# State-space stage of a graph network: its turns written out, and the order of work inside a turn changed

## The chip, the cores and the metric

The kernel is one program on one core of a Trainium2 chip. The metric is device time in microseconds (us) from launch to end. The engines are named as in the profile: PE is TensorE (matmuls), PEld its weight loads, DVE is VectorE, ACT is ScalarE, POOL is GpSimd, SP is SyncE, which here issues the DMAs. They run on their own and meet at semaphores.

## The reference, cut to what matters

The whole computes eight layers over 128 graphs of 40 nodes with 128 features. The change touches the second one, `L0_ffn`, alone: nodes are gathered softly into 64 slices, the slices go through a state-space model that runs in both directions, and come back to the nodes.

```python
fx = (x @ W_fx.T + b_fx)                       # per head: 8 heads of 64
xm = (x @ W_x.T + b_x)
sw = softmax((xm @ W_slice.T + b_slice) / temp)    # node -> slice weights ("logits", softmax)
snorm = sw.sum(2)                                  # slice sums
st = einsum('bhnc,bhng->bhgc', fx, sw) / (snorm + 1e-05)[..., None]
# _hydra(st): input projection, convolution, silu, two scans along the 64 slices
#   h = h * dA_t + dBx_t ; y_t = h . C_t           (written as weights W = decays * (B.C) here)
y  = y + x_og * repeat(x_og @ fcD_w.T + Dp, P)
yg = y * silu(z)
yg = yg * rsqrt(mean(square(yg)) + 1e-05) * norm_w # square sums, root, scales
ot = yg @ out_w.T                                  # output projection
out = einsum('bhgc,bhng->bhnc', ot, sw)            # back to the nodes
x = x + out @ out_w.T + out_b                      # to features
```

## The kernel before

`l0_ffn` (L1947) works on 16 chunks (`NCH`) of 8 graphs. In a chunk there are 4 pairs of graphs (`CHP`); a chunk's slices are 512 columns. Three chunks are in work at a time: turn c ends chunk c, takes chunk c+1 through the middle, and begins chunk c+2. Turns run from -2 to 15, so there are 18. `all_turns` (L2153) writes turns -2, -1, 14 and 15 out and has the other fourteen in a hardware loop of seven passes, each with an even and an odd turn in its body; every engine has this loop and a branch at its end (L2156). In the loop, chunk numbers in semaphore waits are register values.

Each engine does the steps of a turn in a fixed order, its list `turn`. TensorE's is:

1. `slices(c+1)`: 128 small matmuls (L2254), 16 transposes of the softmax weights (L2246), which ScalarE copies out (L2401);
2. `input_projection(c+1)`: 10 groups of 4 matmuls (L2280 the first, then L2278); it waits until VectorE has scaled all states (`states`, L2531, semaphore `u_out`) and ScalarE made half of its copies;
3. `mix(c)` (L2320), `steps_down(c+1)` (L2291, L2293), `gains(c+1)` (L2301, L2302; the B-C products), `logits(c+2)` (L2225, L2226);
4. `squares(c)` (L2328), which waits for VectorE's square sums; `output_projection(c)` (L2338), four groups q of 4 matmuls into banks 4 and 5 in turn, of which group 2 waits for ScalarE's copy 0 and group 3 for copy 1 (L2467);
5. `slice_sums(c+2)` (L2239), which waits for the end of the softmax (`smd`); `back_to_nodes(c)` (L2350), `dt_down(c+1)` (L2307), `to_features(c)` (L2358).

VectorE's: `states(c+1)`, the scans (`decayed`, `weights`) of chunk c, `convolve(c+1)`, `gate(c)` (L2591), `square_sums(c)` (L2596, L2598; it waits for ScalarE's squares), `biases(c+2)` (L2498, L2499; each pair waits for its logits), `scales(c)` (L2602; waits for the root), `softmax(c+2)` (maximum L2506, subtraction L2508, then, after ScalarE's exponentials, sum L2510, reciprocal, product L2514), `inverses(c+2)` (L2519, L2521; waits for the slice sums), `nodes(c)`, `out(c)` (L2612; waits for to_features), `columns(c+1)`.

ScalarE's: `slices`, `projected`, `steps_down` of c+1, then `squares(c)` (L2452), `root(c)` (L2456), `out_copy(c, 0)`, `exps(c+2)` (L2392), `out_copy` 1 to 3, `nodes(c)`.

SP's: `load_xn`, `spread_decays(c+1)`, `spread_inverses(c+2)`. The last writes the inverses of the slice sums to memory in 4 DMAs (L2190) and, once these are there, reads them back spread over the partitions in 8 (L2196); `states` of the next turn waits for these pair by pair.

Of the kernel before, what the change touches and what calls it, by code (L numbers as in the profile page):

```python
# [9 lines left out]
ALU = mybir.AluOpType  # L10
# [1936 lines left out]
def l0_ffn(nc, g):  # L1947


    with nc.cleanup_on_exit(), ExitStack() as ctx:  # L1950
# [193 lines left out]
        def there(k):  # L2144

            return not isinstance(k, int) or 0 <= k < NCH
# [4 lines left out]
                eng.wait_ge(sem, value)  # L2151

        def all_turns(eng, turn):  # L2153
            turn(-2, 0)
            turn(-1, 1)
            with eng.Fori(0, (NCH - 2) // 2) as i:  # L2156
                turn(2 * i, 0)
                turn(2 * i + 1, 1)
            turn(NCH - 2, 0)
            turn(NCH - 1, 1)  # L2160

        block = ctx.enter_context(nc.Block())

# [44 lines left out]
        def _(pe):  # L2208
# [19 lines left out]
            def slice_sums(k):  # L2228

                pe.wait_ge(s["smd"], k + 1)  # L2230
                wait(pe, s["xt_out"], 4 * k)
                if there(k - 2):
                    pe.wait_ge(s["ot_out"], 4 * (k - 2) + 3)
                for par in range(2):
                    for f in range(2):
                        o = PS[4][32 * (2 * par + f):32 * (2 * par + f + 1), 0:2 * SG].rearrange("p (k n) -> p k n", k=2)
                        for q in range(CHP):
                            rhs = sw[:, q, :].rearrange("p (f k a n) -> p f a k n", f=2, a=2, n=SG)[:, f, par]
                            mm = pe.matmul(o, selS[:, q, :], rhs, start=(q == 0), stop=(q == CHP - 1))  # L2239
                mm.then_inc(s["sn_ps"], 1)  # L2240
# [87 lines left out]
                    mm = pe.matmul(PS[7][:, 448 + q:449 + q], sq[:, 0, q * 128:(q + 1) * 128], g.mean_w[:, 0:1], start=True, stop=True)  # L2328
                mm.then_inc(s["r_ps"], 1)

            def output_projection(k):
                if there(k + 1):
                    pe.wait_ge(s["xt_out"], 4 * k + 8)
                for q in range(CHP):
                    if q >= 2:
                        pe.wait_ge(s["ot_out"], 4 * k + q - 1)
                    for t in range(KT):
                        mm = pe.matmul(PS[4 + q % 2][:], yg[:, t, q * 128:(q + 1) * 128], wo[:, t, :], start=(t == 0), stop=(t == KT - 1))  # L2338
                    mm.then_inc(s["ot_ps"], 1)
# [12 lines left out]
                    mm.then_inc(s["o_ps"], 1)  # L2352

            def to_features(k):
                pe.wait_ge(s["oT_out"], 2 * k + 2)
                pe.wait_ge(s["oT_act"], 2 * k + 2)
                for t in range(KT):
                    mm = pe.matmul(PS[6][:, 0:CH], wout[:, t, :], oT[:, t].rearrange("p q j n -> p (q j n)"), start=(t == 0), stop=(t == KT - 1))  # L2358
                mm.then_inc(s["f_ps"], 1)

            def turn(c, par):
                if there(c + 1):
                    slices(c + 1)
                    input_projection(c + 1)
                if there(c):
                    mix(c)
                if there(c + 1):
                    steps_down(c + 1)
                if there(c + 1):
                    gains(c + 1)  # L2370
                if there(c + 2):
                    logits(c + 2)
                if there(c):
                    squares(c)
                    output_projection(c)
                if there(c + 2):
                    slice_sums(c + 2)
                if there(c):
                    back_to_nodes(c, par)
                if there(c + 1):  # L2380
                    dt_down(c + 1)
                if there(c):
                    to_features(c)
# [3 lines left out]
        def _(act):  # L2387
# [75 lines left out]
            def out_copy(k, q):  # L2463
                act.wait_ge(s["ot_ps"], 4 * k + q + 1)
                if q == 0:
                    act.wait_ge(s["rms"], k + 1)
                act.activation(ot[:, q, :], PS[4 + q % 2][:], ACT.Copy, scale=rms[:, q:q + 1]).then_inc(s["ot_out"], 1)  # L2467

            def turn(c, par):
                if there(c + 1):  # L2470
                    slices(c + 1, 1 - par)
                    projected(c + 1, 1 - par)
                if there(c + 1):
                    steps_down(c + 1)
                if there(c):
                    squares(c)
                    root(c)
                    out_copy(c, 0)
                if there(c + 2):
                    exps(c + 2)  # L2480
                if there(c):
                    for q in range(1, CHP):
                        out_copy(c, q)
                    nodes(c)
            all_turns(act, turn)
# [2 lines left out]
        def _(dve):  # L2488
# [10 lines left out]
                    dve.tensor_tensor(fx[:, q, :], PS[2 + q % 2][:], bfx[:], ALU.add).then_inc(s["lg_out"], 1)  # L2499
                dve.drain()  # L2500

            def softmax(k):

                sw3 = sw[:].rearrange("p q (h n) -> p (q h) n", n=SG)
                bc = sst[:, :, None].broadcast_to([128, CHP * SH_, SG])
                dve.tensor_reduce(sst[:], sw3, AX.X, ALU.max)  # L2506
                dve.drain()
                dve.tensor_tensor(sw3, sw3, bc, ALU.subtract).then_inc(s["smx"], 1)  # L2508
                dve.wait_ge(s["sme"], k + 1)
                dve.tensor_reduce(sst[:], sw3, AX.X, ALU.add)  # L2510
                dve.drain()
                dve.reciprocal(sst[:], sst[:])
                dve.drain()
                dve.tensor_tensor(sw3, sw3, bc, ALU.mult).then_inc(s["smd"], 1)  # L2514

            def inverses(k):

                dve.wait_ge(s["sn_ps"], k + 1)
                dve.tensor_scalar(rn[:], PS[4][:, 0:2 * SG], 1e-5, None, ALU.add)  # L2519
                dve.drain()  # L2520
                dve.reciprocal(rn[:], rn[:]).then_inc(s["rn"], 1)  # L2521

# [77 lines left out]
            def scales(k):  # L2600
                dve.wait_ge(s["rt"], k + 1)
                dve.reciprocal(rms[:], rms[:]).then_inc(s["rms"], 1)  # L2602
# [25 lines left out]
            def turn(c, par):  # L2628
                if there(c + 1):
                    states(c + 1)  # L2630
                if there(c):
                    decayed(c, 0)
                if there(c + 1):
                    dt_ready(c + 1)
                if there(c):
                    dve.drain()
                    decayed(c, 1)
                    weights(c)
                if there(c + 1):
                    convolve(c + 1)  # L2640
                if there(c):
                    gate(c, par)
                    square_sums(c)
                if there(c + 2):
                    biases(c + 2)
                if there(c):
                    scales(c)
                if there(c + 2):
                    softmax(c + 2)
                if there(c + 2):  # L2650
                    inverses(c + 2)
                if there(c):
                    nodes(c)
                    out(c)
                if there(c + 1):
                    columns(c + 1)
# [98 lines left out]
```

## Time and profile before

| | us |
|---|---|
| three runs | 3872.6, 3874.0, 3877.59 |
| median | 3874.0 |
| the profiled execution | 3859.76 |
| its span, first to last instruction | 3857.9 |
| mean granted TensorE clock | 0.871 |

The page gives, for each engine, its busy time and its share of the span, then the span in 40 slices with a digit for each engine, and the granted clock of TensorE (PEclk, tenths of 2.4 GHz). A slice is 96.4 us; turns 0 to 14 of the state-space stage lie in the fifth to the sixteenth or so. A matmul of 32-bit numbers has two records here, so a row "x8" of 128x512 matmuls is one group of four. In the order of time and in the table of groups, the idle time in square brackets or behind the bar is that just before the instruction, with what ended it; "issue" is time in which the engine waited for nothing that the profile shows.

### The profile page before, as it was taken

To read this page: it belongs to the slowest core of one execution; us is meant where nothing else is said; L and a number is where in the kernel's file an instruction comes from. 1 tells how busy PE (TensorE), PEld (TensorE's weight loads), DVE (VectorE), ACT (ScalarE), POOL (GpSimd) and SP (SyncE) were. 2 spreads that over 40 slices of the span, in tenths; PEclk is the share of its full clock that TensorE was granted. 3 is DMA by queue.
4 is the path that set the end of the run, shared out by engine and by line. 5 is a ranking of instruction groups with operands and counts; after the bars stand their busy time and mean duration, and the time that the engine had idled before them with its cause. 6 is when DMAs were issued, how large, how long until landed. Compare 5 with 4: busy or idle time off the path is not lost. (4 is left out here: it accounts for less than half of the span.)

```text
span 3857.9 us, 56708 instructions
## 1 busy us (share of the span) xinstructions
PE 3137.0 (81%) x21385; PEld 1980.1 (51%) x21385; DVE 2420.5 (63%) x4174; ACT 1336.8 (35%) x2519; POOL 234.5 (6%) x196
## 2 busy tenths in 40 slices
PE   6357999999999999535549995789885988986998
PEld 5224555555555555324426663556552655653665
DVE  6636767777767776399673334488895345773333
ACT  3223434344434344110434443312111444543444
POOL 0000000000000000000000000033221004320000
PEclk7678999999999999755769997699997987897999
DMA  3121121112111112100013321000000212102322
GB/s 38 48 82 37 37 51 37 37 38 59 37 40 48 37 37 51 46 13 1 29 32 78 78 55 15 5 1 0 1 0 26 69 39 51 41 22 58 75 68 68
DMA packets 145000, 152.62 MB, mean 40 GB/s; under 512 B 66628, under 2 KB 124896, under 8 KB 142328
## 3 DMA queue, kind: packets, MB, share of 16 engines
q1 hardware_dynamic: 144800, 149.72, 16.0%
q8 instruction: 154, 2.52, 0.3%
q14 instruction: 46, 0.38, 0.0%
HBM read 141.26 MB, written 8.44 MB: 39 GB/s over the span
## 5 line engine op out<-in xcount | busy, mean ns | idle before, releaser
L812 DVE TENSOR_TENSOR f_hg<-f_hs,f_gb 128x640 f32<-128x640 f32 x320 | 263.7, 825 | 507.6 <-ACT f_hs L794 448.5
L2278 PE MATMUL hy_ps<-hy_uT,hy_win 128*128 128x512 f32 x1152 | 498.7, 594 | 0.0
L794 ACT ACTIVATE f_hs<-f_ph,f_b1t 128x320 f32<-128x320 f32 x640 | 335.1, 527 | 406.2 <-PE f_ph L762 402.2
L762 PE MATMUL f_ph<-XNP,f_w 128*128 (+1 forms) x1280 | 404.8, 440 | 12.9 <-PEq L644 8.6
L777 PE MATMUL f_po<-f_hg,f_w 128*128 128x320 f32 x1280 | 404.9, 439 | 8.9 <-DVE f_hg L812 8.9
L2278 PEld LDWEIGHTS hy_ps<-hy_uT,hy_win 128*128 128x128 f32 x1152 | 217.6, 190 | 281.2 <-issue 281.2
L762 PEld LDWEIGHTS f_ph<-XNP,f_w 128*128 128x128 f32 x1280 | 247.3, 194 | 117.5 <-issue 18.8
L777 PEld LDWEIGHTS f_po<-f_hg,f_w 128*128 128x128 f32 x1280 | 240.4, 191 | 126.4 <-issue 21.3
L2338 PE MATMUL hy_ps<-hy_wo,hy_yg 128*128 128x512 f32 x512 | 227.4, 603 | 0.0
L1803 PE MATMUL er_c<-XNG 128*128 128x400 f32 x544 | 204.6, 516 | 22.4 <-POOL XNG L1734 22.1
L1748 ACT ACTIVATE er_OT<-er_t 128x384 bf16<-128x384 f32 x128 | 61.1, 490 | 309.1 <-PE er_t L1773 309.1
L2338 PEld LDWEIGHTS hy_ps<-hy_wo,hy_yg 128*128 128x128 f32 x512 | 97.7, 193 | 117.0 <-issue 117.0
L2544 DVE TENSOR_TENSOR_SCAN XNG<-XNG,hy_fx 128x2048 f32<-128x2048 f32 x32 | 141.6, 4425 | 2.9 <-issue 1.1
L1783 PE MATMUL er_g<-er_TP,er_OT 128*128 128x320 bf16 x768 | 133.0, 312 | 10.5 <-ACT er_OT L1748 6.1
L1803 PEld LDWEIGHTS er_c<-XNG 128*128 128x128 f32 x544 | 98.7, 194 | 83.0 <-POOL XNG L1734 25.5
L1734 POOL TENSOR_TENSOR XNG<-er_VW,er_MD 128x400 f32<-128x400 f32 x136 | 122.4, 900 | 296.0 <-DVEq L1704 197.2
L2401 ACT ACTIVATE hy_swT<-hy_ps 64x160 f32<-64x160 f32 x256 | 76.4, 299 | 136.8 <-PE hy_ps L2246 133.4
L236 ACT ACTIVATE n_xt<-n_i 128x512 f32<-128x512 f32 x70 | 40.0, 594 | 219.7 <-PE n_i L199 218.7
L207 PE MATMUL n_o<-ident,n_xt 128*128 128x128 f32 x280 | 54.9, 345 | 71.8 <-DVE n_xt L290 71.7
L199 PE MATMUL n_i<-ident,XT 128*128 128x128 f32 x280 | 49.3, 332 | 78.4 <-PEq L2666 28.0
L2418 ACT ACTIVATE hy_xr<-hy_ps 128x512 f32<-128x512 f32 x80 | 47.5, 594 | 177.1 <-PE hy_ps L2278 177.1
L1094 PEld LDWEIGHTS g_ps<-ident,g_P 40*40 40x40 f32 x2048 | 83.2, 128 | 40.6 <-issue 35.7
(520 smaller groups left out, 5506.6 us busy)
## 6 DMA issues: line engine op xcount, KB each, us to landing
f_gb<-gate_rows SPq DMA_DIRECT2D x32, 1280.0 KB, 8.5
XNG<-hy_decays SPq DMA_DIRECT2D x32, 1024.0 KB, 9.5
hy_rb<-hy_inverse SPq DMA_DIRECT2D x128, 128.0 KB, 3.1
f_gb<-gate_rows SPq DMA_DIRECT2D x16, 640.0 KB, 5.1
g_KB<-g_keys SPq DMA_DIRECT2D x32, 320.0 KB, 4.5
hy_xn<-XNP SPq DMA_DIRECT2D x1, 4096.0 KB, 12.5
hy_XC<-hy_xn SPq DMA_DIRECT2D x16, 256.0 KB, 3.4
XNG<-in_L_ffn_edge_index_dram SPq DMA_DIRECT2D x2, 2048.0 KB
```

The source lines that it names most:

```text
L762: pe.matmul(psh[e % 2][k][:], w1[:, e, k * 128:(k + 1) * 128], chunk_view(g, c), start=True, stop=True).then_inc(h_ps, 1)
L777: mm = pe.matmul(pso[par][:], w2[:, e * H2 + k, :], hg[:, e % 2, k, :], start=False, stop=(e == E - 1 and k == H2 - 1))
L794: ins = act.activation(hs[:, e % 2, k, :], psh[e % 2][k][:], ACT.Gelu, bias=b1t[:, e * H2 + k:e * H2 + k + 1])
L812: dve.tensor_tensor(hg[:, e % 2], hs[:, e % 2], gb[:, par, e, None, :].broadcast_to([128, H2, CH]), ALU.mult).then_inc(hg_ready, 1)
L1094: mm = pe.matmul(pst[n % 2][j][rows(j), h, :], P[rows(j), c % 2, h, q, :], g.ident[rows(j), rows(j)], start=True, stop=True)
L1734: pool.tensor_tensor(X[:, u % XBUF], VW[:, 1 - par, u, :, None].broadcast_to([128, V, TJ]), MD[:, 1 - par, u, None, :].broadcast_to([128, ...
L1783: pe.matmul(o[:, 0:NS], OT[:, u % 2, j, :], TP[:, i, j * NS:(j + 1) * NS], start=(i == 0 and j == 0), stop=(i == 2 and j == J - 1))
L1803: mm = pe.matmul(flat(acc[j][:]), OD[:, 1 - par, u, j * 128:(j + 1) * 128], flat(X[:, u % XBUF]), start=False, stop=False, skip_group_chec ...
L2278: mm = pe.matmul(p[:], win[:, t, m * 128:(m + 1) * 128], uT[:, t, :], start=(t == 0), stop=(t == KT - 1))
L2338: mm = pe.matmul(PS[4 + q % 2][:], yg[:, t, q * 128:(q + 1) * 128], wo[:, t, :], start=(t == 0), stop=(t == KT - 1))
L2401: ins = act.activation(o, p[:, :, j, 0:N], ACT.Copy)
L2544: dve.tensor_tensor_scan(L[:, a][:, st], dAb[:, a][:, st], E[:, st], 0.0, ALU.mult, ALU.add)
```

## The change

All turns are written out, and the loop is gone. On TensorE `logits(c+2)` goes ahead of `gains(c+1)`; `output_projection` takes a range of groups, and `slice_sums(c+2)` stands between its third group and its last; the sums go to bank 6 instead of 4, so they no longer wait for the output copies, and `to_features`, which writes bank 6, waits for the inverses (`rn`). On ScalarE the exponentials go ahead of all four output copies. On VectorE `biases(c+2)` goes ahead of `square_sums(c)`, and `scales(c)` stands inside the softmax, after its subtraction. No operation is added or left out.

```diff
         def all_turns(eng, turn):
-            turn(-2, 0)
-            turn(-1, 1)
-            with eng.Fori(0, (NCH - 2) // 2) as i:
-                turn(2 * i, 0)
-                turn(2 * i + 1, 1)
-            turn(NCH - 2, 0)
-            turn(NCH - 1, 1)
+            for c in range(-2, NCH):
+                turn(c, c % 2)
@@ TensorE, slice_sums
                 wait(pe, s["xt_out"], 4 * k)
-                if there(k - 2):
-                    pe.wait_ge(s["ot_out"], 4 * (k - 2) + 3)
-                        o = PS[4][32 * (2 * par + f):32 * (2 * par + f + 1), 0:2 * SG].rearrange("p (k n) -> p k n", k=2)
+                        o = PS[6][32 * (2 * par + f):32 * (2 * par + f + 1), 0:2 * SG].rearrange("p (k n) -> p k n", k=2)
@@ TensorE, output_projection
-            def output_projection(k):
+            def output_projection(k, groups):
-                for q in range(CHP):
+                for q in groups:
@@ TensorE, to_features
+                if there(k + 2):
+                    pe.wait_ge(s["rn"], k + 3)
@@ TensorE, turn
+                if there(c + 2):
+                    logits(c + 2)
                 if there(c + 1):
                     gains(c + 1)
-                if there(c + 2):
-                    logits(c + 2)
                 if there(c):
                     squares(c)
-                    output_projection(c)
+                    output_projection(c, range(CHP - 1))
                 if there(c + 2):
                     slice_sums(c + 2)
                 if there(c):
+                    output_projection(c, range(CHP - 1, CHP))
                     back_to_nodes(c, par)
@@ ScalarE, turn
                     root(c)
-                    out_copy(c, 0)
                 if there(c + 2):
                     exps(c + 2)
                 if there(c):
-                    for q in range(1, CHP):
+                    for q in range(CHP):
@@ VectorE, softmax and inverses
-            def softmax(k):
+            def softmax(k, meanwhile):
                 dve.tensor_tensor(sw3, sw3, bc, ALU.subtract).then_inc(s["smx"], 1)
+                meanwhile()
                 dve.wait_ge(s["sme"], k + 1)
-                dve.tensor_scalar(rn[:], PS[4][:, 0:2 * SG], 1e-5, None, ALU.add)
+                dve.tensor_scalar(rn[:], PS[6][:, 0:2 * SG], 1e-5, None, ALU.add)
@@ VectorE, turn
                     gate(c, par)
-                    square_sums(c)
                 if there(c + 2):
                     biases(c + 2)
                 if there(c):
+                    square_sums(c)
+                if there(c + 2):
+                    softmax(c + 2, lambda: scales(c) if there(c) else None)
+                    inverses(c + 2)
+                else:
                     scales(c)
-                if there(c + 2):
-                    softmax(c + 2)
-                if there(c + 2):
-                    inverses(c + 2)
```

## Rows read from the trace of the kernel before

**Rows 1.** The page: busy time, share of the span, instructions.
```profile
PE 3137.0 (81%) x21385; PEld 1980.1 (51%) x21385; DVE 2420.5 (63%) x4174; ACT 1336.8 (35%) x2519; POOL 234.5 (6%) x196
```

**Rows 2.** Windows, output projection to output projection: busy per engine, clock, DMA.
```profile
383.00:1465.40 1082.40, 1037.28 (x8219) 573.60 (x8218) 792.97 (x899) 432.79 (x767) 0.00 (x0) 0.97 0.17 43
...
883.20:964.20 81.00, 77.58 (x634) 42.77 (x634) 60.87 (x70) 33.30 (x59) 0.00 (x0) 1.00 0.17 44
1048.90:1131.00 82.10, 78.85 (x633) 42.98 (x634) 60.98 (x70) 33.29 (x59) 0.00 (x0) 0.98 0.17 43
```

**Rows 3.** Waits of TensorE, 400 to 1500 us: total, times, longest.
```profile
PE hy_ps L2254 <- issue: 17.6, 12, 1.8
PE hy_ps L2280 <- DVE hy_uT L2531: 14.8, 8, 2.9
PE hy_ps L2246 <- ACT hy_swT L2401: 4.3, 8, 0.5
PE hy_ps L2280 <- ACT hy_swT L2401: 4.2, 5, 1.8
```

**Rows 4.** TensorE in time, boundary after turn 5 (branch): start, duration.
```profile
822.98 1.97 PE L2254 MATMUL hy_ps<-hy_sw,hy_fx 40*64 40x64 f32 x89 [1.25 <-issue]
826.51 1.64 PE L2254 MATMUL hy_ps<-hy_sw,hy_fx 40*64 40x64 f32 x39 [1.56 <-issue]
```

**Rows 5.** TensorE in time, boundary after turn 6 (no branch).
```profile
909.76 0.63 PE L2246 MATMUL hy_ps<-ident,hy_sw 128*128 128x128 f32 x4 [0.54 <-ACT hy_swT L2401]
912.13 3.63 PE L2280 MATMUL hy_ps<-hy_uT,hy_wdt 128*40 128x512 f32 x8 [1.75 <-ACT hy_swT L2401]
```

**Rows 6.** VectorE in time, turn 6 and the states after it.
```profile
875.65 1.23 DVE L2596 TENSOR_TENSOR hy_uT<-hy_uT 128x1024 f32<-128x1024 f32 x1 [4.86 <-ACT hy_uT L2452]
...
883.24 0.68 DVE L2499 TENSOR_TENSOR hy_fx<-hy_ps,hy_bfx 128x512 f32<-128x512 f32 x1
...
890.90 2.29 DVE L2510 TENSOR_REDUCE hy_sst<-hy_sw 128x32 f32<-128x2048 f32 x1 [2.17 <-ACT hy_sw L2392]
...
893.69 2.29 DVE L2514 TENSOR_TENSOR hy_sw<-hy_sw,hy_sst 128x2048 f32<-128x2048 f32 x1
899.65 0.29 DVE L2519 TENSOR_SCALAR hy_rn<-hy_ps 128x128 f32<-128x128 f32 x1 [3.67 <-PE hy_ps L2239]
...
911.33 0.76 DVE L2531 TENSOR_TENSOR hy_uT<-hy_ps,hy_rb 128x256 f32<-128x256 f32 x2 [0.54 <-DMA hy_rb<-hy_inverse]
```

**Rows 7.** TensorE in time, gains to output projection of turn 6.
```profile
872.65 0.33 PE L2301 MATMUL hy_ps<-hy_Cs,hy_xs 64*64 64x64 f32 x4
...
874.90 1.10 PE L2225 MATMUL hy_ps<-hy_wlg,hy_XC 128*128 128x512 f32 x2
...
878.89 1.12 PE L2225 MATMUL hy_ps<-hy_wlg,hy_XC 128*128 128x512 f32 x2 [0.32 <-DVE hy_fx L2499]
...
881.57 1.02 PE L2226 MATMUL hy_ps<-hy_wfx,hy_XC 128*128 128x512 f32 x2
882.43 0.95 PE L2328 MATMUL hy_ps<-mean_w,hy_uT 128*128 128x1 f32 x8
883.24 13.98 PE L2338 MATMUL hy_ps<-hy_wo,hy_yg 128*128 128x512 f32 x32
```

**Rows 8.** ScalarE in time, copies of the transposes after turn 6.
```profile
908.39 4.99 ACT L2401 ACTIVATE hy_swT<-hy_ps 64x160 f32<-64x160 f32 x16 [5.83 <-PE hy_ps L2246]
```

**Rows 9.** Windows (columns as rows 2) where the clock was low.
```profile
825.00:831.80 6.80, 5.28 (x56) 4.68 (x55) 3.85 (x9) 2.45 (x9) 0.00 (x0) 0.50 0.43 135
...
1040.00:1043.40 3.40, 3.40 (x6) 1.32 (x5) 2.73 (x4) 1.41 (x2) 0.00 (x0) 0.51 1.10 231
...
1541.80:1548.60 6.80, 4.59 (x12) 3.04 (x13) 2.10 (x3) 1.68 (x3) 0.00 (x0) 0.50 0.63 130
```

**Rows 10.** TensorE in time, turn 14: squares and what they waited for.
```profile
1544.01 1.86 PE L2328 MATMUL hy_ps<-mean_w,hy_uT 128*128 128x1 f32 x8 [2.65 <-DVE hy_uT L2598]
```

**Rows 11.** TensorE in time, turn -1: slice sums after logits.
```profile
312.95 3.43 PE L2239 MATMUL hy_ps<-hy_sw,hy_selS 128*32 128x128 f32 x26 [13.18 <-DVE hy_sw L2514]
```

## The prediction

> **What bounds the kernel now.** I began with the page: TensorE is busy for 3137.0 of the 3857.9 us span [rows 1], and the slices of the page that belong to the state-space stage are its fullest. Then I read the stage turn by turn, with the busy time by window, each window from one output projection to the next [rows 2]. Thirteen such turns take 1082.4 us, 83.3 each, and TensorE is busy in 1037.28 of them, VectorE in 792.97, ScalarE in 432.79. So TensorE sets the pace. The best turn, 883.2 to 964.2, had clock 1.00 and 77.58 us of matmuls; that is the floor of a turn with the same work. Whatever a turn takes above 77.58 is one of two things: matmuls that ran at the lower clock, 1.2 instead of 2.4 GHz (1037.28 - 13 x 77.58 = 28.7 us in thirteen turns), or time in which TensorE waited. The change moves no arithmetic out of TensorE, so it can only earn or lose in these two.
>
> The table of TensorE's waits says where they are [rows 3]: nearly all lie at the turn's boundary, between to_features and the first input projection. The order of time shows that there are two kinds of boundary. After an odd turn the loop branches back: two stops, 1.25 and 1.56 us, with no releaser but "issue", in the middle of the slices [rows 4]. After an even turn, and after turn 13, where the branch isn't taken, these are absent and other waits stand: 0.54 us before the last transposes (for ScalarE's copies) and 1.75 before the projection [rows 5]. There are 6 boundaries of the first kind and 8 of the second; their four lines in the table add up to 17.6 + 14.8 + 4.3 + 4.2 = 40.9 us.
>
> **Writing the turns out.** The 6 taken branches go. Straight code doesn't stop so: the boundaries of rows 5 are straight code, inside the loop body. What is late next is what rows 5 show, so this edit alone would turn 2.8 us of stop (up to some 4 with what follows) into 2.3; it needs the earlier slice sums to be worth more. The branches of VectorE, ScalarE and SP lie beside TensorE's work, since each of them waits at the boundary anyway (VectorE for the inverses' transfers [rows 6]); none is priced.
>
> The Trainium skill (Advanced Engine Details and Errata, Control Flow Timing) gives some 108 ns for a compare-and-branch; by that, six of them would be worth 0.65 us and this edit nothing. The trace disagrees on TensorE: 1.25 + 1.56 us of stop stand at one branch.
>
> **Slice sums three groups into the output projection.** The 1.75 us wait is the end of a chain: slice sums, then inverses on VectorE (899.65), two hops of DMA, and the last scaled states, which wait for the second hop, at 911.33 + 0.76 = 912.09 [rows 6]; the projection starts at 912.13 [rows 5]. (The row names ScalarE as releaser, but its second copy was done at 910.9, as below; it was the states.) The change starts the chain one projection group earlier. The four groups of one turn take 13.98 us, so one is 3.49 us [rows 7]. The wait of 1.75 (at most 2.91 [rows 3]) is then gone on this side, and the next in line is ScalarE: its 16 copies run from 908.39 to 913.38 [rows 8], so half of them, which the projection needs, are done at 910.88. TensorE arrives at 910.39 (the last transposes start at 909.76 and take 0.63). That leaves 0.54 with the semaphore. VectorE's own order allows it: four pairs of scaled states take 4 x 0.76 = 3.04 us and can begin when out and columns are done, 0.25 us or so before the 906.9 at which they begin now, so they can end at 910.0 (an estimate). So each of 14 boundaries keeps 0.54 + 0.54 = 1.08 us, 15.1 in all: **40.9 - 15.1 = 25.8 us gained**.
>
> The sums' bank goes from 4 to 6, with a new wait in to_features for the inverses. These are ready some 1.3 us after the sums (two operations from 899.65 on), and to_features comes after the last group, back_to_nodes and dt_down, at least 6 us after them: nothing. Behind it would stand the whole next turn, so it is worth naming; it decides only if the inverses were 5 us later. SP issues the same transfers in the same order, only earlier: it waits for the inverses with nothing in front of them.
>
> **Logits ahead of gains, biases ahead of square sums.** Logits start 2.25 us earlier, which is what gains take (872.65 to 874.90), and the 0.32 wait in them goes [rows 7], since VectorE no longer makes the square sums (from 875.65 on) at that moment [rows 6]. But now the square sums stand behind the biases, and squares(c) on TensorE waits for them. Worked out: the last logits end at 881.57 + 1.02 - 2.25 - 0.32 = 880.02 [rows 7]. The last biases end 1.33 us after them (883.24 + 0.68 = 883.92 against 882.59) [rows 6], and the square sums take 1.23 for the first addition, a little over half of that for the second, of half the size, and some 0.2 for drains and semaphores: together 3.5, so 883.5. TensorE has finished gains at 882.43 - 0.32 = 882.1. **A new wait of 1.35 us in each of 14 turns**, less the 0.32: 14 x 1.03 = 14.4 us lost. Queued behind it on TensorE are the whole output projection, the slice sums and so the chain above.
>
> **Softmax, scales, exps.** The softmax starts at 883.5 instead of just after the 883.92 of the biases, and the exponentials no longer stand behind the first output copy and their table load. Its first two operations take 2.3 us each, like the two at 890.90 and 893.69, so ScalarE starts the exponentials at 888.1; its own 1.9 us later, at 890.05 against 890.90 now, VectorE goes on. smd comes at 895.1, not 893.69 + 2.29 = 895.98 [rows 6]. TensorE has three groups done at 884.3 + 10.5 = 894.8. So slice_sums waits 0.3 us when the clock is full and not at all when it fell; I take 0.1, 1.4 us in all. The output copies 0 and 1 come after the exponentials, 890.7 and 891.4; groups 2 and 3 want them at 891.2 and 897: nothing. The reciprocal of scales lies in VectorE's wait for the exponentials (2.17 us there now [rows 6]).
>
> **The clock.** Before a fall TensorE had done little. In rows 9, at 825.00, it had stopped for 1.25 us, worked for 1.97 and stopped again, for 1.56 [rows 4], and it stays 6.8 us at 0.50; at 1040.00, right after gains, it has 3.4 us at 0.51. The row that is nearest to the new wait is in turn 14, which has no logits: gains, then a wait of 2.65 us for the square sums, then squares, and 6.8 us at 0.50 at the start of its output projection [rows 9, 10]. The change makes the same order in every turn, with a wait half as long, followed by 0.9 us of matmuls of one column: 4.5 us of small matmuls and waiting. So I expect the clock to fall once in each turn there, for 3.4 us, part of it in the wait itself. The price: a turn with one short stretch of low clock (clock 0.98, 78.85 us of matmuls) has 1.27 more than the best one, 1.4 or so in other such turns; I take 1.45 for a fall that lies wholly on work, and 1.2 here, since the wait covers some: 14 x 1.2 = 16.8. At the boundary the stops get shorter, 1.08 instead of 2.3 to 3.4, but the transposes between them are short matmuls too, and rows that show such a boundary don't exist; between a fall at each and none I take 3.4 us in 45 of 100: 14 x 0.45 x 1.45 = 9.1. Against 28.7 + 1.7 (turn 13's boundary, 2.91 us of wait) now: **30.4 - 25.9 = 4.5 us gained**. The bounds are wide: the new place from nothing to 2.5 us a turn, the boundary from nothing to 1.45.
>
> The Trainium skill has a rule against the change here (TensorE: Matmul & The Clock Gate, A second HAM failure mode): frequent small idles between groups of matmuls make the clock go up and down. Rows 9 agree that stops of 1.25 and 1.56 us do it, and the sum has its price.
>
> **Before the loop.** In turn -1 TensorE waits 13.18 us between logits and slice sums [rows 11]. Gains, 2.25 us, go into this wait and logits come forward: 2.3 us gained, once. Turn 14 and 15 have no logits and stay as they are.
>
> **The sum**: -25.8 + 14.4 + 1.4 - 4.5 - 2.3 = -16.8 us. The profiled execution took 3859.8 us (span 3857.9); it lies 14 us under the median of the runs, 3874.0, and I take the same difference off that: **3857 us**.
>
> **Rivals.** (1) Forecast: -17, from -26 to -9. Chance 0.55. (2) The clock holds at the new wait: 16.8 less, and at the boundaries up to 9.1 less: -34 to -43, 3840 to 3831 us. For it, the boundary at 904 to 913 of rows 5 had 2.29 us of stops and no fall. Against it, rows 9 at 1541.80. Chance 0.14. (3) Slower: the new wait in front of the output projection brings 6.8 us of low clock in each turn as in turn 14, 2.6 instead of 1.2 us (+19.6), and the boundary keeps its fall every time (+11.2): +14, 3888 us. It decides from some 2.2 us of clock loss a turn at the new place, with the boundary at its worst. Against it, the wait is half of turn 14's. Chance 0.10. (4) The slice sums don't come early, since smd is later than worked out; the 1.85 us stay at all boundaries: 14 x 1.3 = +18, so +1, 3875 us. For it, the margin in the sum is negative (-0.3 us) and VectorE has no slack from the logits to smd. Against it, 3.49 us are there to be eaten. Chance 0.14. (5) The change doesn't do what it says: straight code stops as the loop did, 6 boundaries keep 3.4 us of stop (+14) and 2.5 of clock (+6): +3, 3877 us. Against it, rows 5. Chance 0.07.
>
> **How the numbers follow.** About 0.2% (7.7 us) is what a measurement of this kernel can tell from no change. Faster: (1) and (2), 0.70 rounded. Same: (4) and (5), 0.20. Slower: (3), 0.10. The range from 3840 to 3878 holds (1), (4), (5) and the near half of (2); left out are (3) and the far half of (2).
>
> **What would show it.** No "issue" stop before the slices and the last wait before the input projection put down to ScalarE, 0.5 us, would show the first two steps; a wait of squares for the square sums of 1.3 to 1.4 us in 14 turns, the third; turns of 82 us with 0.97 of clock, each with a fall just before or in the output projection, the fourth; a wait of slice_sums over 1 us would be (4). The prediction is wrong if the clock behaves otherwise at the new wait than it did in turn 14: every other term is a subtraction of rows.

## The result, and the profile after

The changed kernel took 3853.4 us (median of six runs, 3847.6 to 3856.7) against 3871.2 us of the kernel before (six runs, 3866.4 to 3877.6): 17.8 us less, ratio 0.9937 with a 95% interval of 0.9911 to 0.9963. (The two medians alone give 0.9954. That lies inside the interval, which allows 14 to 35 us less; the whole times do not fix the gain more closely than that.) The forecast was 3857 us from a median of 3874.0, 17 us less. In the profiled executions the span went from 3857.9 to 3845.8 us, by 12.1 only; where the rest is comes last in this section.

First the page of the changed kernel, to hold against [rows 1], and the windows of thirteen turns, then one turn, to hold against [rows 2]. The columns are those of [rows 2]; the third row is one turn, the fourth its part of low clock, the fifth what follows up to 1.4 us before its end.

```profile
PE 3141.3 (82%) x21385; PEld 1976.2 (51%) x21385; DVE 2420.4 (63%) x4174; ACT 1336.6 (35%) x2519; POOL 234.7 (6%) x196
```

```profile
380.90:1445.90 1065.00, 1031.50 (x8219) 563.59 (x8218) 791.48 (x898) 432.58 (x767) 0.00 (x0) 0.98 0.18 43
1445.90:1522.80 76.90, 72.82 (x618) 40.80 (x618) 54.73 (x61) 33.27 (x59) 0.00 (x0) 0.97 0.17 42
544.60:626.40 81.80, 79.23 (x634) 43.25 (x633) 60.87 (x70) 33.26 (x59) 0.00 (x0) 0.98 0.18 43
545.70:549.10 3.40, 3.40 (x6) 1.34 (x5) 2.52 (x3) 1.51 (x2) 0.00 (x0) 0.50 0.00 0
549.10:625.00 75.90, 73.86 (x618) 40.42 (x617) 55.84 (x66) 30.86 (x57) 0.00 (x0) 1.00 0.19 47
```

Thirteen turns went from 1082.4 to 1065.0 us. The kinds of turn are gone: eleven of the thirteen take 81.8 us each, and twelve have one fall of the clock, 3.4 us long, that begins 0.4 to 1.3 us into the output projection. In the one turn left it is 6.8 us long and begins before squares. The counts of matmuls are the same, so what changed is the waits and the clock. TensorE's waits by line, 395 to 1480 us (total, times, longest), stand against [rows 3]:

```profile
PE hy_ps L2321 <- DVE hy_uT L2594: 14.9, 13, 1.1
PE hy_ps L2273 <- ACT hy_swT L2397: 8.7, 14, 0.6
PE hy_ps L2239 <- ACT hy_swT L2397: 7.5, 14, 0.5
```

No stop is put down to "issue" any more. Every boundary is now of one kind; in order of time, one of them and, from the same turn, squares with the new wait (TensorE), to hold against [rows 5] and [rows 7]. The wait is alike in all turns; this turn is the one with the long fall, which is why squares take 1.87 us here:

```profile
871.03 1.87 PE L2321 MATMUL hy_ps<-mean_w,hy_uT 128*128 128x1 f32 x8 [1.15 <-DVE hy_uT L2594]
...
901.47 0.63 PE L2239 MATMUL hy_ps<-ident,hy_sw 128*128 128x128 f32 x4 [0.53 <-ACT hy_swT L2397]
902.72 3.60 PE L2273 MATMUL hy_ps<-hy_uT,hy_wdt 128*40 128x512 f32 x8 [0.63 <-ACT hy_swT L2397]
```

The window of that fall, with the clock in the third column from the end:

```profile
870.00:876.80 6.80, 5.77 (x13) 3.56 (x14) 5.47 (x5) 2.78 (x3) 0.00 (x0) 0.50 0.00 0
```

VectorE in the same turn shows the new order, to hold against [rows 6]: the square sums behind the last biases, the softmax without a pause before it, the inverses (887.72) while the last group is still running, and the states in one piece, since they wait for no transfer.

```profile
868.21 0.68 DVE L2494 TENSOR_TENSOR hy_fx<-hy_ps,hy_bfx 128x512 f32<-128x512 f32 x1
868.98 1.23 DVE L2592 TENSOR_TENSOR hy_uT<-hy_uT 128x1024 f32<-128x1024 f32 x1
870.28 0.69 DVE L2594 TENSOR_TENSOR hy_uT<-hy_uT 128x512 f32<-128x512 f32 x1
...
880.30 2.29 DVE L2510 TENSOR_TENSOR hy_sw<-hy_sw,hy_sst 128x2048 f32<-128x2048 f32 x1
887.72 0.29 DVE L2515 TENSOR_SCALAR hy_rn<-hy_ps 128x128 f32<-128x128 f32 x1 [5.13 <-PE hy_ps L2232]
...
898.43 2.74 DVE L2527 TENSOR_TENSOR hy_uT<-hy_ps,hy_rb 128x256 f32<-128x256 f32 x8
```

The output projection of turn 14 begins at 1522.8, and before it began at 1545.7: 22.9 us. Of these the profiled execution gives 10.8 back behind the stage. The graph stage `l3_gnn` (L947), which the change doesn't touch, took 265.2 us instead of 254.1. Its window in the kernel before, in the changed kernel, and in another profile of the changed kernel (e8 below):

```profile
3186.70:3440.80 254.10, 235.92 (x2508) 160.38 (x2509) 178.18 (x161) 126.74 (x278) 101.56 (x32) 0.85 0.16 39
```

```profile
3163.20:3428.40 265.20, 248.35 (x2482) 167.87 (x2482) 178.21 (x161) 125.78 (x275) 101.56 (x32) 0.79 0.15 37
```

```profile
3169.00:3418.30 249.30, 231.48 (x2482) 157.86 (x2482) 178.21 (x161) 125.51 (x276) 101.53 (x32) 0.85 0.15 39
```

VectorE is busy for the same 178.2 us in all three. TensorE's clock in that stage was 0.79 once and 0.85 twice. With one and the same program it takes 249 or 265 us, so the 11 us can't be put down to the change; one execution differs from another by more. From the output projection of turn 14 to the end it takes 2312.2 us in the kernel before, 2323.0 in the changed one, and 2314.3 in e8, the same program again. The runs of one kernel spread over 9 us and more, so the medians are a blunter tool here than thirteen turns read in a trace. Those aren't exact either: two traces of the changed kernel agree within 0.2 us, two of the kernel of e4 and e11 differ by 4.1.

### The profile page after: what moved, and what is told of

It reads as the page before. It is cut to its first block and busy times, and to the rows that moved or that the text cites. A ratio compares the mean times of both kernels' runs of the same rounds, so it can differ in the third digit from the quotient of the medians.

```text
span 3845.8 us, 55739 instructions
## 1 busy us (share of the span) xinstructions
PE 3141.3 (82%) x21385; PEld 1976.2 (51%) x21385; DVE 2420.4 (63%) x4174; ACT 1336.6 (35%) x2519; POOL 234.7 (6%) x196
## 5 line engine op out<-in xcount | busy, mean ns | idle before, releaser
L2331 PE MATMUL hy_ps<-hy_wo,hy_yg 128*128 128x512 f32 x512 | 255.8, 659 | 0.0
L1783 PE MATMUL er_g<-er_TP,er_OT 128*128 128x320 bf16 x768 | 131.2, 309 | 10.1 <-ACT er_OT L1748 6.1
```

The lines of the kernel that those rows point to most:

```text
L1783: pe.matmul(o[:, 0:NS], OT[:, u % 2, j, :], TP[:, i, j * NS:(j + 1) * NS], start=(i == 0 and j == 0), stop=(i == 2 and j == J - 1))
```

## The experiments

The theory is that of the prediction: the branch's stops and the chain of the slice sums were the waits at the boundary; the new wait of squares and the fall of the clock at it are what the change pays. The rivals are (2) to (5). All ratios are to the kernel before, run on the same chip: one chip for e1 to e4, a second for e5 to e8, a third for e9 to e11. Differences in us between kernels are those of their medians, and a few us between kernels run on different chips are not to be relied on. Not tried alone are the exponentials ahead of the copies, the scales inside the softmax and the other bank of the slice sums. For comparison, the thirteen turns from output projection to output projection, read in each trace:

| kernel | ratio, 95% interval | median us | 13 turns us |
|---|---|---|---|
| before | 1 | 3871.2 to 3874.8 | 1082.4 |
| changed | 0.9937 (0.9911 to 0.9963) | 3853.4 | 1065.0 |
| e1 changed, with the loop | 1.0045 (1.0025 to 1.0065) | 3890.1 | 1105.5 |
| e2 before, written out | 0.9993 (0.9976 to 1.0010) | 3871.6 | 1078.7 |
| e3 changed, slice sums late | 1.0070 (1.0046 to 1.0093) | 3903.9 | 1109.7 |
| e4 square sums between biases | 0.9857 (0.9831 to 0.9883) | 3825.0 | 1037.6 |
| e5 changed, wait filled | 0.9938 (0.9915 to 0.9961) | 3851.1 | 1064.2 |
| e6 changed, old order | 0.9939 (0.9918 to 0.9960) | 3853.5 | 1064.9 |
| e7 e4, gains inside the projection | 0.9880 (0.9855 to 0.9906) | 3828.7 | 1036.4 |
| e8 changed again | 0.9944 (0.9922 to 0.9965) | 3851.6 | 1064.8 |
| e9 e4, gains spread | 0.9837 (0.9818 to 0.9856) | 3816.1 | 1031.6 |
| e10 e9, first transposes early | 0.9857 (0.9842 to 0.9872) | 3821.1 | 1025.2 |
| e11 e4 again | 0.9851 (0.9828 to 0.9874) | 3818.3 | 1041.7 |

### e1: the loop put back into the changed kernel

```diff
-            for c in range(-2, NCH):
-                turn(c, c % 2)
+            turn(-2, 0)
+            turn(-1, 1)
+            with eng.Fori(0, (NCH - 2) // 2) as i:
+                turn(2 * i, 0)
+                turn(2 * i + 1, 1)
+            turn(NCH - 2, 0)
+            turn(NCH - 1, 1)
```

> The changed kernel with the hardware loop put back; all other edits stay. Theory: the six taken branches stop TensorE for 1.25 + 1.56 us each, where straight code with early slice sums has 0.53 + 0.62, and each brings 6.8 us of low clock (2.4 us lost) where straight code has none: 6 x (1.7 + 2.4) = 25 us slower than the changed kernel. Rival (a branch costs some 0.1 us and the stops come from elsewhere): within 2 us of the changed kernel, and no stop with the releaser issue.

37 us slower than the changed kernel, where 25 were expected, and slower than the kernel before. TensorE's waits, 400 to 1500 us, and the thirteen turns, with one turn that ends at a branch:

```profile
PE hy_ps L2252 <- issue: 21.9, 12, 2.4
```

```profile
385.20:1490.70 1105.50, 1057.22 (x8218) 583.75 (x8218) 790.67 (x898) 433.24 (x767) 0.00 (x0) 0.95 0.17 42
467.40:555.20 87.80, 82.58 (x634) 46.42 (x634) 61.77 (x70) 33.27 (x59) 0.00 (x0) 0.93 0.17 41
```

The stops are back, 21.9 us at six branches, 3.6 each, more than in the kernel before (17.6). The rest of the loss is clock: 1057.22 us of matmuls against 1031.50. Each of the six branches brings a fall of 6.8 us, and in the turn behind it the fall at the new wait is 6.8 us long too, where the changed kernel has 3.4. The records of the branch itself on TensorE's sequencer, in the kernel before and in e1 (shortest, median and longest of seven, in ns):

```profile
L2156 PEldq COMPARE_BRANCH  x7: 83/3435/3712, 484.7 to 1484.9; - x7
```

```profile
L2156 PEldq COMPARE_BRANCH  x7: 83/4210/4524, 488.9 to 1512.2; - x7
```

The one of 83 ns is the last, which isn't taken; the six that are taken have 3.37 to 3.71 us in the kernel before and 4.01 to 4.52 in e1. The rival, a branch that costs 0.1 us, is out, and with it that figure of the Trainium skill (Advanced Engine Details and Errata, Control Flow Timing) as a price for a loop on TensorE.

### e2: the kernel before, written out and nothing else

The opposite of e1's edit, on the kernel before.

> The kernel before with its turns written out and nothing else. Theory: six boundaries go from some 3.4 us of stops to the 2.4 of the others (6 us) and from 6.8 us of low clock to 3.4 (6 x 1.2 = 7 us): 13 us faster than before, so most of the whole change's 18; the last wait before the input projection is for the scaled states in all 14. Rival: the writing out alone is worth nothing, because the chain of the slice sums is next in line: within 3 us of before.

No difference in whole time; the thirteen turns are 3.7 us shorter. The theory's 13 us were wrong, and the rival was right: the chain of the slice sums is next in line. The waits, 400 to 1500 us, say how:

```profile
PE hy_ps L2275 <- DVE hy_uT L2526: 31.2, 13, 3.8
PE hy_ps L2241 <- ACT hy_swT L2396: 7.5, 14, 0.5
...
PE hy_ps L2275 <- ACT hy_swT L2396: 1.8, 1, 1.8
```

31.2 + 7.5 + 1.8 = 40.5 us, against 40.9 in [rows 3]. Each branch's stop is gone, and a wait of the same sum for the scaled states stands in its place: 1.6 to 2.2 us at ten boundaries, 3.2 to 3.8 at four. At the four, the first hop of the inverses was late. SP's queue at a late one and at an ordinary one (start, duration of the issues; the second hop is issued as soon as the first has landed):

```profile
568.40 1.29 SPq L2185 DMA_DIRECT2D hy_inverse<-hy_rn  x4
572.38 1.73 SPq L2191 DMA_DIRECT2D hy_rb<-hy_inverse  x3
```

```profile
653.92 1.29 SPq L2185 DMA_DIRECT2D hy_inverse<-hy_rn  x4
656.20 2.37 SPq L2191 DMA_DIRECT2D hy_rb<-hy_inverse  x4
```

3.98 us against 2.28. In e2 a transfer of instructions falls into the first hop at every boundary, late or not (the DMA queues from 568.4 to 572.4 us: packets, MB, share):

```profile
q8 instruction: 1, 0.02, 2.0%
```

In the changed kernel it falls behind the first hop in thirteen of the fourteen turns, and there no hop took over 2.50 us. In e2 it is there at the ordinary hops too, so it can't be the whole reason for a late one; what makes a hop late stays open. The kernel before has late hops as well, four in turns 0 to 13 (5.17, 3.77, 5.22 and 3.41 us); the last of them is the 2.91 us wait of [rows 3].

### e3: the slice sums after all four groups again

```diff
-                    output_projection(c, range(CHP - 1))
+                    output_projection(c, range(CHP))
                 if there(c + 2):
                     slice_sums(c + 2)
                 if there(c):
-                    output_projection(c, range(CHP - 1, CHP))
                     back_to_nodes(c, par)
```

> The changed kernel with the slice sums after all four groups of the output projection. Theory: the wait before the input projection goes from 0.62 back to some 1.8 us (14 x 1.2 = 17 us) and the clock falls at each boundary again (14 x 1.4 = 20 us): 17 to 37 us slower than the changed kernel, so slower than before. Rival: the chain was not what TensorE waited for: within 3 us.

50 us slower than the changed kernel by the medians and 44.7 in the thirteen turns, more than both ends of what was expected.

```profile
PE hy_ps L2273 <- DVE hy_uT L2526: 29.8, 13, 4.0
```

```profile
381.50:1491.20 1109.70, 1053.17 (x8218) 573.45 (x8218) 794.54 (x898) 433.00 (x767) 0.00 (x0) 0.95 0.17 42
```

The chain is what TensorE waits for, with three late hops among them as in e2 (longest wait 4.0), and the matmuls take 21.7 us longer (1053.17 against 1031.50) because ten of the thirteen boundaries have a fall again and the fall at the wait of squares is 6.8 us long in five turns instead of one. The early slice sums are the edit that carries the change. The 3.49 us by which they come earlier are more than the ordinary wait of 1.8 needs. Whether they would cover a late hop isn't shown, since the changed kernel had none.

### e4 and e11: square sums between biases 1 and 2

```diff
-            def biases(k):
+            def biases(k, meanwhile):
                 for q in range(CHP):
+                    if q == CHP // 2:
+                        meanwhile()
@@ turn
-                    biases(c + 2)
-                if there(c):
+                    biases(c + 2, lambda: square_sums(c) if there(c) else None)
+                else:
                     square_sums(c)
```

> The changed kernel with VectorE's square sums between biases 1 and 2 instead of behind all four. Theory: squares on TensorE no longer wait (14 x 1.15 = 16 us), and if it is this wait that makes the clock fall at the start of the output projection, 14 x 1.7 = 24 us more: 16 to 40 us faster than the changed kernel. Rival (the clock falls because of gains and squares themselves, wait or none): 16 us. Second rival (the softmax then ends later and slice sums wait instead): within 3 us.

28 us faster than the changed kernel, faster than both kernels by their intervals. Waits, 395 to 1450 us, and thirteen turns:

```profile
PE hy_ps L2273 <- ACT hy_swT L2397: 8.8, 14, 0.6
PE hy_ps L2239 <- ACT hy_swT L2397: 7.5, 14, 0.5
...
PE hy_ps L2232 <- DVE hy_sw L2512: 3.8, 8, 0.8
```

```profile
381.40:1419.00 1037.60, 1015.21 (x8219) 556.89 (x8218) 788.86 (x898) 432.78 (x767) 0.00 (x0) 0.99 0.18 44
```

Squares don't wait; instead the slice sums wait for the softmax, 0.4 us in seven turns and 0.8 in one. Waits fell by 11 us and matmul time by 16.3: eight turns have no low clock at all and 77.46 us of matmuls, five have one fall of 3.4 us behind gains and squares. So the fall went with the wait of squares in most turns, and in some it came without the wait.

> The run with the square sums between biases 1 and 2 once more, unaltered, as the measure of the other two on the same chip: 0.985 to 0.988 of the kernel before.

0.9851, within the range expected. In its trace the thirteen turns take 4.1 us more than in e4's: six have a fall, two of them 6.8 us long. The number of falls is thus not fixed by the program.

### e5: the wait filled with a matmul

```diff
             def squares(k):
+                if there(k + 1):
+                    pe.wait_ge(s["xt_out"], 4 * k + 8)
+                if there(k + 2):
+                    pe.matmul(PS[5][:], yg[:, 0, 0:128], wo[:, 0, :], start=True, stop=True)
                 pe.wait_ge(s["sq_sum"], k + 1)
```

> The changed kernel with one more 128x512 matmul per turn (0.86 us, its result used by nothing) issued into the 1.15 us wait in front of squares. Theory: the clock falls there because TensorE stands still between gains and squares; with two thirds of the wait filled it falls in few turns, so up to 14 x 1.75 = 24 us faster than the changed kernel, although the work grew. Rival: the fall belongs to gains and squares, or follows any stretch without long accumulations; then it stays in every turn and the time is the same within 3 us.

Nothing gained; the rival was right. In order of time, the filler and squares, TensorE:

```profile
459.99 1.10 PE L2322 MATMUL hy_ps<-hy_wo,hy_yg 128*128 128x512 f32 x2
461.28 1.86 PE L2325 MATMUL hy_ps<-mean_w,hy_uT 128*128 128x1 f32 x8 [0.18 <-DVE hy_uT L2598]
463.00 3.76 PE L2335 MATMUL hy_ps<-hy_wo,hy_yg 128*128 128x512 f32 x4
```

The wait is 0.18 us and the clock falls nevertheless, now for 6.8 us in every second turn. One matmul in the wait isn't enough; the theory that standing still is the cause is out in that simple form. That the falls go with the whole stretch from the first of gains to the last of squares would fit, and no run shows it apart.

### e6: gains and square sums back in their old places

```diff
-                if there(c + 2):
-                    logits(c + 2)
                 if there(c + 1):
                     gains(c + 1)
+                if there(c + 2):
+                    logits(c + 2)
@@ VectorE
+                if there(c):
+                    square_sums(c)
                 if there(c + 2):
                     biases(c + 2)
-                if there(c):
-                    square_sums(c)
```

> The changed kernel with gains ahead of logits and square sums ahead of biases again; written out, early slice sums and early exponentials stay. Theory: no wait of squares (1.15 us less, 0.32 for biases more) and no fall of the clock in most turns (1.75 less); but the softmax starts at 884.1 instead of 883.5 while TensorE has three groups done at 893.7, so slice sums wait for it, some 1.5 us: 14 x (1.15 - 0.32 + 1.75 x 0.8 - 1.5) = 10 us faster than the changed kernel. Rival (the reorder is what makes the early slice sums possible): slower than the changed kernel by over 5 us.

The same time as the changed kernel, so neither the theory's 10 us nor the rival's. Waits, 400 to 1485 us:

```profile
PE hy_ps L2331 <- ACT XNP L2463: 11.5, 13, 0.9
PE hy_ps L2232 <- DVE hy_sw L2510: 11.3, 13, 1.2
```

The wait of squares is gone, and 0.88 us in the output projection (for copy 0, which stands behind the exponentials) and 0.87 for the softmax took its place; the falls are in 5 of 13 turns, and begin with the last of gains, as the one at 1040.00 in [rows 9] does, where no wait is near. The nine executions spread over 37 us, and the profiled one is the longest. I had seen the second wait, not the first. The reorder of logits and biases, one of the edits of the change, was therefore worth nothing in a turn: it paid with the wait of squares and its fall what it saved on the softmax and the copy.

### e7 and e9: gains inside the output projection

Both stand on top of the edit of e4. e7 moves gains(c+1) behind group 1 of output_projection(c), with a wait for the root (`rt`), which reads the same bank. e9 spreads the pairs:

```diff
                     squares(c)
-                    output_projection(c, range(CHP - 1))
+                    for q, pairs in enumerate(((0,), (1, 2), (3,))):
+                        output_projection(c, range(q, q + 1))
+                        if there(c + 1):
+                            if q == 0:
+                                pe.wait_ge(s["rt"], c + 1)
+                            gains(c + 1, pairs)
```

> Square sums between biases 1 and 2, and on TensorE gains moved between groups 1 and 2 of the output projection, so that squares follow the logits and nothing small stands beside them. Theory: the falls of the clock that are left in the run with the square sums between the biases (5 of 14 turns, 1.6 us each) go, the waits stay (0.42 for the softmax, 1.16 at the boundary): 8 us faster than that run. Rival: squares now come too early for the square sums, 0 to 1 us of wait per turn, and the time is the same as of that run or up to 14 us more.

The 8 us didn't come: the thirteen turns are 1.2 us shorter than e4's, and the whole time isn't less. The falls didn't go: 4 of the 13 turns have one, and it moved with gains. TensorE in one such turn and the window behind it:

```profile
624.51 0.33 PE L2294 MATMUL hy_ps<-hy_Cs,hy_xs 64*64 64x64 f32 x4
...
626.51 0.39 PE L2295 MATMUL hy_ps<-hy_wfd,hy_xs 128*128 128x8 f32 x2
626.76 5.38 PE L2331 MATMUL hy_ps<-hy_wo,hy_yg 128*128 128x512 f32 x8
```

```profile
627.50:630.90 3.40, 3.40 (x5) 1.35 (x4) 3.04 (x3) 0.00 (x0) 0.00 (x0) 0.51 0.00 0
```

Gains stand between long matmuls without any wait, and within 1 us of them the clock is at 0.51 for 3.4 us; 8 records of the projection take 5.38 instead of 3.68 us. They are enough on their own, in some turns.

> As the run with the square sums between biases 1 and 2, but the four pairs of gains are spread over the output projection: pair 0 behind group 0, pairs 1 and 2 behind group 1, pair 3 behind group 2. Theory: each fall of the clock follows gains standing together (5 of 14 turns there, 4 of 14 with gains in one piece inside the projection, 1.6 us each); spread, they bring none: 6 to 8 us faster than the run with the square sums between the biases. Rival: matmuls of that size cost clock wherever they stand; same time as that run within 3 us.

```profile
376.90:1408.50 1031.60, 1010.08 (x8219) 551.09 (x8218) 788.90 (x898) 431.37 (x767) 0.00 (x0) 1.00 0.18 45
```

No fall in any of the thirteen turns (clock 1.00), every turn but one 79.32 us. The turns are 6.0 us shorter than e4's and 10.1 than e11's; the ratio, 0.9837, is the best measured, but its interval overlaps that of e11 (0.9828 to 0.9874), run on the same chip 2.2 us slower by the median, so the whole time doesn't separate the two. e10, with gains spread in the same way, has no fall in its thirteen turns either.

### e8 and e10

> The changed kernel once more, unaltered. Its state-space stage should take the same time as in the first profile, 81.8 us a turn, within 1 us over all turns; what differs between the two profiles should lie in the stages behind it, above all in the last graph stage (l3_gnn), which took 11 us more in the changed kernel's first profile than in that of the kernel before, with 34 us more of low clock.

1064.8 us for the thirteen turns, against 1065.0, as expected. The 249.3 us of `l3_gnn` are shown in the section on the result.

> As the run with gains spread, and the first of the four groups of transposes goes ahead of the small matmuls of slices, so that ScalarE's copies, which TensorE waits for with 0.53 and 0.62 us at each boundary, start 1.8 us earlier. Theory: both waits go, and as the states on VectorE now start 0.9 us later, 0.5 us of wait for them takes their place: 14 x 0.65 = 9 us faster than the run with gains spread. Rival: the states are as late as the copies are early, and the time is the same.

```profile
PE hy_ps L2274 <- ACT hy_swT L2403: 7.5, 14, 0.5
...
PE hy_ps L2285 <- ACT hy_xs L2440: 3.4, 13, 0.5
```

e10 is e9 with the first group of transposes ahead of the small matmuls of slices. One of the two waits at the boundary went, the other stayed, and steps_down now waits 0.2 to 0.5 us for ScalarE. The thirteen turns are 6.4 us shorter than e9's, the whole time isn't (3821.1 against 3816.1 us); in its profile turn 0 came 4.9 us later, and what follows the output projection of turn 14 took 11.0 us more. The edit reaches one or two boundaries in each of these; the cause stays open.

## Why the prediction was right

**The stops and the chain.** Forecast: 40.9 us of waits at 14 boundaries become 15.1. Measured: 8.7 + 7.5 = 16.2. The last wait is put down to ScalarE and is 0.62 us, where 0.54 was forecast. e1 and e3 show that each of the two edits is needed. What failed here is a sentence about the first edit alone: it was to bring 2.8 (some 4) to 2.3 us, and e2 brought 40.9 to 40.5. I had taken the wait behind a straight boundary from one row, 1.75 us; with the chain last at every boundary it is 2.4 on average, for the late hops count each time.

**The wait of squares.** Forecast 1.35 us in 14 turns, measured 1.15; the waits for the biases (0.32) are gone. The square sums ended 3.4 us after the last logits, 3.5 were worked out, and gains began 0.1 us later than the row gave.

**Slice sums.** 0.1 a turn was taken for the softmax, none was measured: the fall of the clock in the first group, forecast in the same paragraph, lets TensorE come late enough every time. Rival (4) is out. e4, where the fall is absent in eight turns, has the 0.4 us.

**The clock.** The size of the sum was nearly right, its parts were not. Forecast: 16.8 us lost at the new wait and 9.1 at the boundaries, 25.9, so 4.5 gained. Gained were 6.9, which leaves 23.5, all of it at the new wait. Measured: a turn has 79.26 us of matmuls against 77.58, 1.68 lost at the new wait, in place of 1.2, and no fall at any boundary, in place of 45 in 100; the thirteen turns have 1031.50 - 13 x 77.58 = 23.0 us, before it was 28.7. The price of 1.2 was mis-sized: I had let the wait cover some of the slow stretch, but in twelve of thirteen turns it begins in the output projection and lies on work whole. Only in the turn shown above it begins in the wait, 1.0 us before squares. That an error of 6.7 us here and one of 9.1 at the boundaries nearly cancel is luck. Rival (3) has its place right and its length wrong: 6.8 us of low clock came in one turn of thirteen. Rival (2) was right for the boundaries.

**Before the loop.** Forecast: 2.3 us from the wait of 13.18 in [rows 11]. It is 10.87 us now, but little of that arrived: from the first logits of turn -2 (208.53, now 207.06) to the output projection of turn 0 it takes 173.9 us instead of 174.5. The new wait of squares in turn 0 takes 1.15 us of it, and the matmuls of that stretch take 0.7 us longer.

**Rival (5)** is out: written out, TensorE has no stop with the releaser "issue".

**The sum.** -24.7 (boundaries), +12.6 (14 x 1.15 less 3.5), -6.9 (5.8 of matmul time in thirteen turns, 1.1 in the next: 73.94 against 72.82 us), -2.3: -21.3, against -16.8 forecast and 21.0 us by which the stage is shorter in the trace (its first instruction comes 1.9 us earlier too). Of those 21.0, 20.8 lie between the output projections of turns 0 and 14. The terms give 19.9 there (24.7 + 6.9 + 3.2 for the biases - 13 x 1.15); 1.1 us that steps_down waited for ScalarE in the kernel before are gone too, and to_features waits 0.2 us more. So the turns are accounted for, and the 2.3 before the loop are not in the result. The medians moved by 17.8. That this is nearer to the forecast than the trace's figure is chance: what lies behind differs by 10 us from one execution to the next.

## What to carry to other kernels

Where an engine sets the pace and two chains end at the same wait, removing one can bring nothing: writing the turns out alone (e2) gave 0 us, and all the other edits without it (e1) +18, with the price of the reorder in it; both together gave -18. Give the second chain its slack first, and count its late cases, here a hop of 3.4 to 5.2 us instead of 2.3 in four of fourteen turns. When a step is moved up so that another engine's work comes later, look for a place in the middle of what it was moved past; here half of the reorder (e4) was worth 28 us more than the whole. Small matmuls of a dense stage are worth spreading between long ones: twenty-six turns of e9 and e10 have no fall, though the gain in whole time isn't clear of the noise.

## What the runs showed of the hardware

- A taken branch of a long loop body stops TensorE for 2.4 to 3.9 us here, in two pieces, and 6.8 us at half clock go with it (10.2 once). Its own record is 3.4 to 4.5 us; the same branch not taken has 83 ns. The Trainium skill (Runtime: NRT & Kernel Launch, Instruction fetch mechanics) says that a taken branch to a far target must fetch instructions first; the stops of e1, and their absence in the straight code, agree.
- The clock falls behind 2.25 us of gains with no wait near them (e7: 0.51 for 3.4 us), and falls although a wait is filled (e5). With the same matmuls spread there is no fall in thirteen turns each of e9 and e10. The Trainium skill's rule on small idles between groups of matmuls (TensorE: Matmul & The Clock Gate, A second HAM failure mode) agrees with the wait of squares, but e7 shows a fall behind small matmuls without an idle.
- A fall of 3.4 us costs 1.3 to 1.7 us: 1.3 to 1.6 where it falls behind the boundary (kernel before, e2), 1.4 in the logits (e6) and 1.6 to 1.7 in the output projection (a turn of e4 with a fall has 79.09 us of matmuls, one without 77.46).
- The two hops of small transfers through memory took 2.28 us for the first in most turns, and 3.8 to 4.1 in four of fourteen in e2 and in e3, where they were last in the chain.
